# A decoder layer on one core: queries loaded one unit sooner, first output rows in halves of one slot, the last unit's step in front of its turns, another order at the head of the last stage

## The reference, cut to what matters

```python
x = x + attn(layernorm(x), Wq, Wk, Wv, Wo)        # 32 heads, 8 key heads, head size 128, rope, causal softmax
x = x + fake_quant(layernorm(x)) @ fake_quant(ctx)
x = x + experts(layernorm(x))                     # 64 experts of rank 8, the best 16 gated by a softmax
```

## Time and profile before

| what | value |
|---|---|
| median of 3 runs | 1272.51 us |
| the runs | 1271.96, 1275.98, 1272.51 us |
| the profiled execution's own time | 1273.53 us |
| its span, first to last instruction | 1271.8 us |
| PE, PE weight load, DVE, ACT, POOL busy | 98%, 84%, 67%, 62%, 48% |
| granted TensorE clock, mean | 1.000 |
| HBM | 147.4 MB read, 88.1 MB written |

### The profile page before, as it was taken

The page is one execution under the profiler, slowest core; times in us unless marked ns, Lnnn a source line. Parts: engine busy times, 40 slices in busy tenths (PEclk is TensorE's granted clock), DMA queues, the critical chain, the costliest instruction groups (busy, mean ns, idle before and its releaser), DMA issues. The chain is left out here.

```text
span 1271.8 us, 19740 instructions
## 1 busy us (share of the span) xinstructions
PE 1248.8 (98%) x6831; PEld 1073.2 (84%) x6831; DVE 850.8 (67%) x1919; ACT 787.3 (62%) x1601; POOL 611.8 (48%) x450
## 2 busy tenths in 40 slices
PE   9999999999999999999999998999999999999998
PEld 8898898888888888888888887878888888868787
DVE  7874735566666667666666766655786777988863
ACT  6412247677767777777777878873333367766530
POOL 4776766678767877778677755520000000021100
PEclk9999999999999999999999999999999999999999
DMA  8043144454857958649486588759964567401111
GB/s 281 18 138 128 59 158 158 148 167 140 240 151 209 247 166 237 170 119 229 142 228 178 129 227 266 210 186 269 294 186 129 165 207 258 147 3 34 50 43 50
DMA packets 122402, 208.72 MB, mean 164 GB/s; under 512 B 15408, under 2 KB 56368, under 8 KB 118720
## 3 DMA queue, kind: packets, MB, share of 16 engines
q1 hardware_dynamic: 118272, 178.10, 42.9%
q0 software_dynamic: 4032, 29.36, 12.2%
HBM read 147.40 MB, written 88.08 MB: 185 GB/s over the span
## 5 line engine op out<-in xcount | busy, mean ns | idle before, releaser
L1342 DVE TENSOR_TENSOR pT_lo<-banks,pT_hi 128x512 fp32r<-128x512 f32 (+1 forms) x192 | 103.6, 595 | 116.0 <-ACT pT_hi L1048 116.0
L1791 PE MATMUL banks<-ob_hi,oa_hi 128*128 128x512 f32 x384 | 149.4, 389 | 0.0
L1791 PE MATMUL banks<-ob_lo,oa_hi 128*128 128x512 f32 x384 | 149.4, 389 | 0.0
L1791 PE MATMUL banks<-ob_hi,oa_lo 128*128 128x512 f32 x384 | 149.4, 389 | 0.0
L1749 PE MATMUL banks<-xc,nring_hi_a 128*128 128x512 f32 x448 | 138.5, 390 | 0.7 <-DVE q_made L1283 0.3
L1749 PE MATMUL banks<-xc,nring_hi_b 128*128 128x512 f32 x448 | 138.6, 391 | 0.0
L1032 ACT CAST oa_hi<-oraw 128x1024 fp32r<-128x1024 f32 x48 | 50.4, 1051 | 127.0 <-PE banks L1791 116.3
L2006 POOL TENSOR_TENSOR resid<-resid,colterm 128x1024 f32<-128x1024 f32 x8 | 19.9, 2491 | 205.4 <-ACT colterm L2064 132.6
L1048 ACT CAST pT_hi<-banks 128x512 fp32r<-128x512 f32 (+1 forms) x192 | 86.5, 527 | 44.8 <-PE banks L1714 44.1
L1697 PE MATMUL banks<-kT,q_hi 128*128 128x512 f32 (+2 forms) x384 | 104.2, 352 | 0.0
L775 POOL TENSOR_TENSOR q_lo<-q_raw,q_hi 128x512 fp32r<-128x512 f32 x64 | 88.9, 1390 | 30.3 <-ACT q_hi L986 30.2
(11 more groups left out here) (275 smaller groups left out, 3405.1 us busy)
## 6 DMA issues: line engine op xcount, KB each, us to landing
q_raw<-qk_dram SPq DMA_DIRECT2D x64, 256.0 KB, 3.9
o_S<-o_st SPq DMA_DIRECT2D x64, 256.0 KB, 3.2
w<-in_L_attn_Wo SPq DMA_DIRECT2D x32, 512.0 KB, 6.4
oraw<-o_S SPq DMA_DIRECT2D x32, 512.0 KB, 4.1
nraw<-in_L_attn_Wq SPq DMA_DIRECT2D x28, 512.0 KB, 6.2
o_S<-o_S POOLq DMA_DIRECT2D x12, 1024.0 KB, 9.7
o_S<-o_N POOLq DMA_DIRECT2D x12, 1024.0 KB, 10.3
resid<-in_x SPq DMA_DIRECT2D x16, 512.0 KB, 7.0
```

The costliest lines, as they stand in the source:

```text
L1342: nc.vector.tensor_tensor(pT[1][:, sl], turned_chunk(turned, mixed, c), as32(pT[0][:, sl]), ALU.subtract).then_inc(pT_lo, 1)
L1791: ins = nc.tensor.matmul(step_bank(m, t), oa[a][:, s % 2, k, t * P:(t + 1) * P], ob[c][:, s % 2, k, :], start=(q == 0 and k == 0 and i == ...
```

## The change

It has five parts.

1. **Queries.** `load_q(v)` of a unit v moves from the start of SP's iteration v-2 into iteration v-3, behind the narrow loads and ahead of `keep_out`, for every v for which `whole_early(v)` holds: 4 to 9, 11 to 49, 51 to 57, 59 and 60.
2. **First rows.** `oraw` slot 0 holds the rows of all first steps, in two halves of 256 columns; the steps of the output projection start in slot 1. `load_first(1)` moves directly behind `load_first(0)`, and its wait is now that of load 0 (the read of job 110 in place of that of job 111).
3. **`first_high`.** For f = 0 the weight is cast before the rows. `first_high(14)` moves between `exps(63)` and `normalise_wide(63)` on ACT, and PE's `first_step(14)` moves ahead of `turn_probs(63)`. First step 15 and DVE's order there stay.
4. **The last job.** In unit 56 DVE does the first addition of job 111 (`begin_last`) behind the reciprocals and ahead of `add_pair(55)`; the two rope products stay behind it.
5. **The last stage's head.** PE turns `a` 4 and the quantised rows 2 ahead of `multiply(1)` (they stood behind it, rows 2 behind `a` 6). ACT does `high("a", 4)` and `copy_turned(2)` ahead of `scale_tile(3)`, and `read_product(1)` ahead of `normalise(0)`. DVE does `quantise(2)` and `row_term(1)` ahead of `add_product(0)`, `low("a", 3)` ahead of `product_stats(0)` and `low("a", 4)` ahead of `scale_of(0)`.

```diff
+    def first_rows(f):
+        return oraw[:, 0, :, (f % 2) * 256:(f % 2) * 256 + 256]
+    def step_rows(s):
+        return oraw[:, (s + 1) % 2, :, :]
...
             if f < 2:
-                sp.wait_ge(job_read, 6 * NARROW - 1 + f)
+                sp.wait_ge(job_read, 6 * NARROW - 1)
...
+        def whole_early(v):
+            return 4 <= v < 8 or 8 <= v < UNITS and (v - 4, 0) in JOB_AT and turning_job(v) <= JOB_AT[v - 4, 0]
         for u in range(1, UNITS):
-            tight = u + 2 < UNITS and (u - 1, 0) in JOB_AT and JOB_AT[u - 1, 0] == turning_job(u + 2)
-            if u + 2 < UNITS and not tight:
+            late = u + 2 < UNITS and not whole_early(u + 2)
+            tight = late and (u - 1, 0) in JOB_AT and JOB_AT[u - 1, 0] == turning_job(u + 2)
+            if late and not tight:
                 load_q(u + 2)
             if u == LAST_JOB_UNIT:
                 load_first(0)
+                load_first(1)
...
-            if u == LAST_JOB_UNIT:
-                load_first(1)
+            if whole_early(u + 3):
+                load_q(u + 3)
...
         def first_high(f):
             q = f % PAIRS
-            act.wait_ge(o_in[f % 2], 16 * (f // 2 + 1))
...
-            nc.scalar.copy(oa[0][:, f % 2, :, 0:256], oraw[:, f % 2, :, 0:256]).then_inc(fa_hi, 1)
             act.wait_ge(w00_in[q // 4], 64)
-            nc.scalar.copy(ob[0][:, f % 2, :, :], w00[:, 2 * q:2 * q + 2, :]).then_inc(fb_hi, 1)
+            if f == 0:
+                nc.scalar.copy(ob[0][:, f % 2, :, :], w00[:, 2 * q:2 * q + 2, :]).then_inc(fb_hi, 1)
+            act.wait_ge(o_in[f % 2], 16 * (f // 2 + 1))
+            nc.scalar.copy(oa[0][:, f % 2, :, 0:256], first_rows(f)).then_inc(fa_hi, 1)
+            if f:
+                nc.scalar.copy(ob[0][:, f % 2, :, :], w00[:, 2 * q:2 * q + 2, :]).then_inc(fb_hi, 1)
...
             exps(u)
+            if u == UNITS - 1:
+                first_high(STEP_AT[UNITS, 0])
             normalise_wide(u)
...
+        def begin_last(j):
+            e, b = j // 7, job_bank(j)
+            dve.wait_ge(job_done, j + 1)
+            dve.wait_ge(job_read, 6 * e + 4)
+            dve.wait_ge(turn_made, 2 * e + 1)
+            link(nc.vector.tensor_tensor(b, b, n_u[:, 0, :], ALU.add))
...
             if u not in SHORT:
                 normalise(u)
+            if u == LAST_JOB_UNIT:
+                begin_last(JOBS - 1)
             if 0 < u <= PAIRED and u % 2 == 0:
                 add_pair(u - 1)
...
             place(u, 1)
+            if u == UNITS - 1:
+                place(UNITS, 0)
             turn_probs(u)
-        place(UNITS, 0)
         place(UNITS, 1)
         mix(UNITS - 1)
```

The three orders of the last stage's head (ACT, DVE, PE):

```diff
         high("k", 0)
+        high("a", 4)
+        copy_turned(2)
         scale_tile(3)
         root(0)
+        read_product(1)
         normalise(0)
-        high("a", 4)
-        read_product(1)
         act.wait_ge(mT_done, 1)
         nc.scalar.copy(mT[0], mb.rearrange("p (k e) -> p k e", e=EXPERTS)).then_inc(mT_hi, 1)
         highs("a", range(5, 8))
-        copy_turned(2)
...
         lows("a", range(3))
+        quantise(2)
+        row_term(1)
         add_product(0)
-        product_stats(0)
         low("a", 3)
         low("k", 0)
+        product_stats(0)
+        low("a", 4)
         scale_of(0)
-        row_term(1)
-        quantise(2)
-        low("a", 4)
         low("a", 5)
...
         multiply(0)
         turn_fill("a", 3)
         turn_fill("k", 0)
+        turn_fill("a", 4)
+        turn_quantised(2)
         multiply(1)
-        turn_fill("a", 4)
         router_matrix()
-        turn_fills("a", range(5, 7))
-        turn_quantised(2)
-        turn_fill("a", 7)
+        turn_fills("a", range(5, 8))
```

More of the change, by code:

```diff
@@ L592, in load_first @@
             q, half = f % PAIRS, f // PAIRS
-            sp.dma_start(oraw[:, f % 2, :, 0:256],
+            sp.dma_start(first_rows(f),
                          o_dram["A00"][2 * q:2 * q + 2, :, half * 256:half * 256 + 256].rearrange("k p c -> p k c")
@@ L610, in load_step @@
                     sp.wait_ge(o_kept[n % 2], o_count(n))
-            sp.dma_start(oraw[:, s % 2, :, :], o_dram[name][2 * q:2 * q + 2].rearrange("k p c -> p k c")
+            sp.dma_start(step_rows(s), o_dram[name][2 * q:2 * q + 2].rearrange("k p c -> p k c")
                          ).then_inc(o_in[s % 2], 16)
@@ L840, in first_low @@
             pool.wait_ge(fa_hi, f + 1)
-            nc.gpsimd.tensor_tensor(oa[1][:, f % 2, :, 0:256], oraw[:, f % 2, :, 0:256],
+            nc.gpsimd.tensor_tensor(oa[1][:, f % 2, :, 0:256], first_rows(f),
                                     as32(oa[0][:, f % 2, :, 0:256]), ALU.subtract).then_inc(fa_lo, 1)
@@ L1031, in step_high @@
                 act.wait_ge(step_done, s - 1)
-            nc.scalar.copy(oa[0][:, s % 2, :, :], oraw[:, s % 2, :, :]).then_inc(oa_hi, 1)
+            nc.scalar.copy(oa[0][:, s % 2, :, :], step_rows(s)).then_inc(oa_hi, 1)
             if m == 0:
@@ L1144, in _ @@
                 narrow_high(j)
-            if (u + 1, 0) in STEP_AT:
+            if (u + 1, 0) in STEP_AT and u + 1 < UNITS:
                 first_high(STEP_AT[u + 1, 0])
@@ L1323, in read_job @@
             else:
-                dve.wait_ge(job_read, 6 * e + 4)
-                dve.wait_ge(turn_made, 2 * e + 1)
-                link(nc.vector.tensor_tensor(b, b, n_u[:, 0, :], ALU.add))
+                if not begun:
+                    begin_last(j)
                 job_turned(b, q_made[:, 0, :], q_made[:, 1, :])
@@ L1388, in step_low @@
             dve.wait_ge(oa_hi, s + 1)
-            nc.vector.tensor_tensor(oa[1][:, s % 2, :, :], oraw[:, s % 2, :, :], as32(oa[0][:, s % 2, :, :]),
+            nc.vector.tensor_tensor(oa[1][:, s % 2, :, :], step_rows(s), as32(oa[0][:, s % 2, :, :]),
                                     ALU.subtract).then_inc(oa_lo, 1)
@@ L1563, in _ @@
             if (u, 0) in JOB_AT:
-                read_job(JOB_AT[u, 0])
+                read_job(JOB_AT[u, 0], u == LAST_JOB_UNIT)
             if (u, 2) in JOB_AT:
```

## The result

The changed kernel takes a median of **1276.68 us** (1274.98 to 1279.59, 22 runs) against 1274.37 us for the kernel before in 22 runs on the same chips: a ratio of **1.0022, 95% interval 1.0013 to 1.0030**. It is slower by 1.7 to 3.8 us, where the prediction had 0.8 us faster. The profiled execution took 1275.85 us (span 1274.1), against 1273.53 (1271.8) before: +2.3 us. Of the 5.0 us between the predicted and the measured median, 1.9 us are the base: the three runs shown had a median of 1272.51 us, the 22, with these three among them, 1274.37. The other 3.1 us are the change's own.

What follows compares the result with a forecast made beforehand. PE was taken as the bound, busy 1248.8 of 1271.8 us, leaving at most 23 us to win. The terms -1.3 + 1.1 - 0.6 = -0.8 us gave a median of 1271.7 us, range 1269.4 to 1274.0 us.

Steps and rivals of the forecast that it cites:

- Queries sooner, unit 56: Turn of unit 56: earlier queries end ACT's wait and start the cast of turned probabilities sooner, -1.4 us (-0.67 to -1.55).
- Every other unit at nothing: All other units: PE does not wait for a query, and a unit's slack covers SP's new wait; cost nothing.
- The fourth rival: SP's new wait each iteration makes `keep_out` late; 0.1 us a unit would give 1277.9 us; chance 0.03.
- Step 0 and step 1: First output projection steps: offset -0.8 us at step 0, half the gain given back, then -1.0 us at step 1.
- First place -1.3 us: Units 54 to 58: step 3's rows load sooner, -1.3 us for the whole place, carried to unit 63.
- Unit 63 +1.1 us: Step 15 waits for DVE's low weight behind the probabilities; PE idle about 2.9 us, +1.1 us (0.9 to 1.6).
- the third rival: Unit 63's pause drops PE's clock, costing 2.0 us: 1273.7 us, or 1275.7 if twice as long; chance 0.07.
- Head -0.6 us: Last stage's head: ACT reaches the router matrix 0.5 us sooner, so `x` 0 turns sooner, -0.6 us (0 to -1.8).

Runs made afterwards that it cites:

- e1: Changed kernel with the queries again loaded one unit later, in their old place; ratio to the kernel before 1.0014.
- e4: Kernel before, queries loaded where they were, plus SP's wait for POOL's low parts of unit u + 1 ahead of the stores of unit u - 2; ratio 0.9993.
- e2: Changed kernel with the early query load issued behind the stores of two units before, not ahead; ratio to the kernel before 1.0002.
- e5: Changed kernel with step 14 and ACT's copies for it back behind the turns of unit 63; ratio to the kernel before 1.0008.
- e11: Kernel before with only the queries one unit sooner, their load behind the stores of two units before; ratio 0.9990.
- e7: Changed kernel with ACT's copies for step 0 in the old order, rows before weight; ratio to the kernel before 1.0020.
- e8: Changed kernel with the old orders at the head of the last stage on ACT, DVE and PE; ratio to the kernel before 1.0022.
- e6: Changed kernel with DVE making step 15's weight low ahead of the low parts of unit 63's probabilities; ratio to the kernel before 0.9993.
- e9: Changed kernel with early queries behind the stores and step 15's weight low ahead of unit 63's probability low parts; ratio to the kernel before 0.9975.
- e10: Changed kernel with queries behind stores, step 15's weight low first and step 0's rows cast first; median 1269.58 us, ratio to the kernel before 0.9964.
- e12: Changed kernel with queries behind stores, step 15's weight low first, step 0's rows cast first, and the last stage's old head; ratio to the kernel before 0.9981.
- e3: Kernel before with only the queries one unit sooner, their load ahead of the stores; ratio 1.0008.

## Why the prediction was wrong

**Queries sooner, unit 56: right.** -1.4 us predicted, -1.54 measured, with no wait in unit 54. But it is the price of one execution's landing: in e1 most of it was there without the change, in e4 0.35 us.

**Every other unit at nothing: this step failed.** It named the wait in front of `keep_out` and excused it by when the stores are *issued*. What counts is when they have *landed*: the slot is free for ACT only then. The step took the landing time as fixed, when it was 4.1 to 5.5 us in the old place and 8.0 to 13.5 us in the new one, and did not count the query's bytes ahead of the stores in the same queue. The cost was 3.2 us in three units in the profile (0.4 to 3.6 us in those of the other five kernels with this order), 2.5 us by e2's ratio. The fourth rival had the mechanism, with a chance of 0.03 and a price spread over all units; it shows in three of 64.

**Step 0 and step 1: direction right, size off.** -0.8 and -1.0 us predicted, 1.61 - 2.79 = -1.18 and 1.25 - 2.79 = -1.54 measured. Against unit 56 the swap of ACT's copies costs step 0 0.4 us, not 0.6: POOL's `first_low(0)` took 1.80 us, between the two values of rows 6. DVE's `lo` of the weight ran beside it, from 767.12 to 768.35 us, and POOL's piece, begun at 767.68 us, ended 1.13 us after that, about what it takes alone (1.29 us). So it made little headway while DVE's ran.

**First place -1.3 us: near.** 2.79 to 1.20 is -1.6 us. With the 2.79 us taken off, step 3's rows were issued at 771.66 us, 0.4 us sooner than the 772.1 predicted, and they landed in 5.2 us, inside the 4.5 to 5.8 taken. In other profiles the step from unit 56 to 58 was -1.96 us (e5) to +0.5 us (e11), so how near this came is partly luck.

**Unit 63 +1.1 us: right, and the pause too.** +1.24 us, with a wait of 2.90 us where 2.9 was worked out, for DVE's `ob_lo` behind the probabilities.

**What that pause does to the clock was the third rival,** at a chance of 0.07. The argument against it, that pauses up to 1.3 us show nothing, says nothing of 2.9 us. Of the five kernels with the pause (changed, e1, e2, e7, e8) 18 of 67 executions had a clock of 1.000; of the five without it (e5, e6, e9, e10, e12) 51 of 53. The chips don't explain that: on the chip of e5, e6, e7 and e9, 7 of 12 executions with the pause were below 1.000 against 1 of 35 without it, on that of e8 and e10 11 of 12 against none of 9. Where in an execution the clock fell, only the profiles say: behind the pause in two of five (e1, e8). There it cost 1.6 us (e1) and 2.8 us (e8), against 2.0 us priced. The Trainium skill, TensorE: Matmul & The Clock Gate, section "What's actually happening", has the rule that the clock falls after idleness; e1 and e8 agree, and the changed kernel's own profiled execution, at 1.00 throughout, does not show it. So the difference of 2.3 us between the profiles holds nothing of the clock, while 16 of the changed kernel's 22 executions have a mean below 1.000.

**Head -0.6 us: mis-sized.** PE's wait fell from 1.25 to 0.70 us and the net is -0.28 us. Against the column sum (+2.61) ACT came to the router matrix 0.27 us sooner (1134.21 against 1131.87 us), not 0.5, and PE's turn followed it.

**Sum.** By the profile -0.4 (up to unit 30) + 3.2 - 1.6 + 1.24 + 0.2 (between step 15 and the column sum) - 0.28, with roundings, is +2.3 us, against the predicted -0.8. The range was too narrow as well: its upper end lies below the median that the kernel before itself had in 22 runs.

Open: why the kernel before, with waits of 1.27 and 0.27 us in unit 63 and the old head, is below 1.000 in 34 of 108 executions (in mean 1.7 us longer than the other 74), when e5 (old unit 63, new head) was so in 0 of 12. e3's profile shows one such fall right behind waits of 1.25 and 0.54 us at the last stage's head. That fits a share of the old head; e12 (new unit 63, old head), below 1.000 in 1 of 9, speaks against it, but weakly, as said there. Both places together, or differences between chips (12 of 35, 9 of 34, 11 of 26 and 2 of 13 for the kernel before), fit as well.

## What to carry to other kernels

An instruction that issues a DMA holds up more than its queue's next issue: price a new wait, or a load put ahead, by when the transfers *behind* it will have landed, not by when they are issued, and put what frees a buffer ahead of what is only wanted later. When a step is moved to fill a gap, look for what its operands still stand behind on each helper engine; here the order of two lines was worth 3.1 us. A new pause of nearly 3 us on TensorE is to be priced with the lower clock behind it, at a chance: a profile can miss it.

## What the runs showed of the hardware

- The same 256 KB stores took 4.1 to 5.5 us to landing from 487 us on (kernel before) and 8.0 to 13.5 us from 492 us on (changed kernel); four identical issues within 2 us differed by up to 5.5 us (8.0 to 13.5).
- Around a pause of 2.90 us the granted clock fell in two of five profiles, 2.0 us after the pause began (e8) and 0.2 us after it ended (e1), and PE then ran at half rate for 3.4 us (e1) or 6 us (e8). Of the executions with this pause 49 of 67 had a mean clock below 1.000, without it 2 of 53.
- Near 340 us ACT waits 1.5 to 3.7 us for a store in 9 of the 14 profiles, in some kernels and not in others with the same orders there (e5 3.71, the changed kernel none; e9 2.35, e10 none). What decides it was not tried; in e2 it made PE 1.9 us late, as much as a whole part of this change.
